# A kernel of attention and a gated feed-forward layer on Trainium2: the product with W2 as seven block products from the second sequence on

## What is computed

```python
# x: (8, 1024, 512) float32; W1, W3: (2048, 512); W2: (512, 2048)
x = x + attention(layernorm(x))        # one head of width 64, causal, rotary, low-rank maps
y = layernorm(x)
hidden = silu(y @ W1.T) * (y @ W3.T)   # 2048 hidden features
hidden = fwht(hidden)                  # Walsh-Hadamard transform over the 2048
x = x + hidden @ W2.T
```

## Time and profile before

| | |
|---|---|
| time, median of 3 runs | 2095.05 us (2094.95 to 2095.1) |
| span of the profiled execution | 2093.3 us |
| around the span, against the median | 1.75 us |
| PE busy | 2049.4 us, 98% |
| DVE busy | 1399.0 us, 67% |
| ACT busy | 932.7 us, 45% |
| POOL busy | 215.0 us, 10% |

### The profile page before, as it was taken

One profiled execution on the slowest core, in us unless ns is written; L12 is line 12 of the kernel. 1 busy time (PEld: TensorE's weight loads), 2 busy tenths in 40 slices (PEclk: granted clock), 3 DMA queues, 4 the chain that ended last, 5 costly groups with the idle time before them and its releaser, 6 DMA issues.

```text
span 2093.3 us, 26809 instructions
## 1 busy us (share of the span) xinstructions
PE 2049.4 (98%) x9846; PEld 986.1 (47%) x9846; DVE 1399.0 (67%) x2674; ACT 932.7 (45%) x1431; POOL 215.0 (10%) x196
## 2 busy tenths in 40 slices
PE   6889999999999999999999999999999999999999
PEld 3534444444444444444444444444444444444444
DVE  7897878667676666766677576766767666743333
ACT  5866455354444444453444444344443445322221
POOL 2354641101001000001001010010100110000000
PEclk8999999999999999999999999999999999999999
DMA  8644246441463333733345423643246332463211
GB/s 336 227 166 174 97 153 153 160 145 60 121 189 111 137 107 95 176 124 116 116 129 161 141 77 106 170 135 130 69 148 154 125 122 92 118 155 108 91 63 68
DMA packets 231138, 278.62 MB, mean 133 GB/s; under 512 B 178016, under 2 KB 178144, under 8 KB 225632
## 3 DMA queue, kind: packets, MB, share of 16 engines
q1 hardware_dynamic: 231008, 276.91, 42.7%
HBM read 194.81 MB, written 39.85 MB: 112 GB/s over the span
## 4 chain that ended last, share of the span: by engine, by line
PE 91%; DVE 4%; ACT 2%; issue 1%; DMA 1%; SPq 0%; POOL 0%; ACTq 0%; DVEq 0%; POOLq 0%
PE PF L926 18%; PE PF L928 17%; PE PF L927 17%; PE PD L988 10%; PE PD L990 10%; PE PD L989 10%; PE XY L747 1%; PE XY L733 1%; PE XY L734 1%; PE XY L757 1%; PE XY L758 1%; PE XY L679 1%; PE XY L678 1%; DMA PT<-Pl 0%; DVE WS L1909 0%
## 5 line engine op out<-in xcount | busy, mean ns | idle before, releaser
L926 PE MATMUL PF<-XF,WS 128*128 128x512 f16 x1778 | 675.3, 380 | 4.1 <-DVE XF L1915 1.9
L928 PE MATMUL PF<-XF,WS 128*128 128x512 f16 x1778 | 673.9, 379 | 0.0
L927 PE MATMUL PF<-XF,WS 128*128 128x512 f16 x1778 | 673.9, 379 | 0.0
L1344 ACT ACTIVATE SH<-PF,afs 128x512 f32<-128x512 f32 x256 | 175.9, 687 | 516.8 <-PE PF L928 514.8
L988 PE MATMUL PD<-W2S,H 128*128 128x512 f16 x1024 | 388.1, 379 | 0.0
L989 PE MATMUL PD<-W2S,H 128*128 128x512 f16 x1024 | 388.1, 379 | 0.0
L990 PE MATMUL PD<-W2S,H 128*128 128x512 f16 x1024 | 388.1, 379 | 0.0
L926 PEld LDWEIGHTS PF<-XF,WS 128*128 128x128 f16 x1778 | 173.8, 98 | 221.6 <-issue 31.0
L928 PEld LDWEIGHTS PF<-XF,WS 128*128 128x128 f16 x1778 | 174.0, 98 | 209.8
L927 PEld LDWEIGHTS PF<-XF,WS 128*128 128x128 f16 x1778 | 174.3, 98 | 186.2 <-issue 4.8
L1950 DVE SCALAR_TENSOR_TENSOR SH<-PF,afs,SH 128x512 f32<-128x512 f32 x256 | 188.8, 747 | 96.8 <-ACT SH L1344 95.0
(11 more groups left out here) (328 smaller groups left out, 2005.2 us busy)
## 6 DMA issues: line engine op xcount, KB each, us to landing
WS<-wscr SPq DMA_DIRECT2D x112, 896.0 KB, 4.9
W2S<-w2scr SPq DMA_DIRECT2D x30, 1024.0 KB, 6.5
ring<-x SPq DMA_DIRECT2D x56, 256.0 KB, 7.1
wscr<-WS SPq DMA_DIRECT2D x16, 896.0 KB, 4.1
out<-ring SPq DMA_DIRECT2D x56, 256.0 KB, 2.3
RAW<-w13t SPq DMA_DIRECT2D x16, 512.0 KB, 4.1
xraw<-xT SPq DMA_DIRECT2D x28, 256.0 KB, 5.4
XF<-w SPq DMA_DIRECT2D x13, 512.0 KB, 18.5
```

The costliest lines, as they stand in the source:

```text
L926: pe.matmul(bank, wh, th, start=i < 2 and j == 0, stop=False, skip_group_check=True)
L927: pe.matmul(bank, wh, tl, start=False, stop=False, skip_group_check=True)
L928: m = pe.matmul(bank, wl, th, start=False, stop=j == 1, skip_group_check=True)
L1344: ac.activation(SH[:, i, :], PF[:, (1 - k % 2, 2)[i], :], ACT.Silu, scale=afs[:, k % NH:k % NH + 1]).then_inc((a_sb, a_sc2)[i], 1)
```

## The change

For the groups of the first sequence (q < `QF` = 4) nothing changes. From q = 4 on the product with W2 is done by seven block products instead of eight. The blocks are: the two hidden tiles of each pair p = k // 2 (q has two pairs, which are two depths of the same sum), the two halves of 512 tokens, and the two halves of 256 features.

- **PE.** `unit(q, u)`, 14 of them for a group (seven products, each for two banks g of 256 tokens), each 12 matmuls of 128x256 with a weight load for each. `UNITS` places three in even steps (positions 1, 3, 6) and four in odd ones (1, 3, 4, 6). A unit waits until the bank of the unit two before it is emptied.
- **Hidden tiles.** The second tile of a pair gets its own buffer SHO (in the space of W2S). `form_sum` on POOL makes four sums of tile halves for a pair, each 128x512, in place; `parts_high` (ACT) and `parts_low` (DVE) split four pieces for a pair, three of 128x1024 and one of 128x512, into H. Before, they split two of 128x1024 for a pair.
- **Results.** Of the 14 units of a group, `take` (ACT) copies 4 into TT, `add_unit` (DVE) adds 4 to TT and 6 to rows of x, and `row_add` (POOL) adds TT to rows, 12 adds of 128x512 in a group. Before, DVE did 8 adds of 128x512 and no other engine had a part in it.
- **W2.** In the first two sequences the sums of W2's blocks are made once (eight rounds of one load, four sums on POOL, one split on ACT and DVE, one store), and `store_w2` issues six more stores each time. From q = 4 on SP loads 256 KB for each of the seven products (three buffers WR) instead of 1 MB for a group.
- **Waits.** `silu` of even steps waits for `parts_low(p - 1, 1)`, the split of the sums, and its second half also for the fourth sum on POOL. Stores of rows come a little later in the sequence.

The core of the diff:

```diff
--- before.py
+++ after.py
+QF = 4
+UNITS = {0: (1, 3, 6), 1: (1, 3, 4, 6), 2: (1, 3, 6), 3: (1, 3, 4, 6)}
+UNIT0 = {0: 0, 1: 3, 2: 7, 3: 10}
+P1, P6, P2, P4, P7, P5, P3 = range(7)
+HFORM = ("A11", "S2", "A12", "A22", "S3", "S1", "S4")
+SPLITS = (("A11", "S3"), ("S1", "S2"), ("A12", "A22"), ("S4",))
+SPLIT_OF = {f: i for i, fs in enumerate(SPLITS) for f in fs}
...
+        SHO = w2s[:, 0:2048].bitcast(F32).rearrange("p (i c) -> p i c", i=2)
+        WR = [w2s[:, o:o + 1024].rearrange("p (r m d) -> p r m d", r=2, m=2) for o in (2048, 3072, 4096)]
+        TT = w2s[:, 5120:7168].bitcast(F32).rearrange("p (g c) -> p g c", g=2)
...
+            def load_form2(n):
+                q, i = QF + n // 7, n % 7
+                if n < 3:
+                    w.wait_ge(p_d, d_no(QF - 2 if n < 2 else QF - 1, 7))
+                else:
+                    w.wait_ge(p_u, 2 * (n - 3) + 2)
+                sp.dma_start(WR[n % 3].rearrange("p r m d -> p (r m d)"), w2f[q % 4, WFILE[i]]).then_inc(d_wf[n % 3], 16)
...
+                    if k > 4 * QF + 3 and unit_at(k, j) and unit_at(k, j)[1] % 2:
+                        n = form_no(unit_at(k, j)[0], unit_at(k, j)[1] // 2) + 3
+                        if n < 7 * (NK // 4 - QF):
+                            load_form2(n)
...
             def down(i):
-                if q < 0:
+                if q < 0 or q >= QF:
...
+            def unit(q, u):
+                i, g, n = u // 2, u % 2, form_no(q, u // 2)
+                bank = PD[:, u % 2, :]
+                w.wait_ge(v_lo, split_no(2 * q + 1, SPLIT_OF[HFORM[i]]))
+                w.wait_ge(d_wf[n % 3], 16 * (n // 3 + 1))
+                if u >= 2:
+                    sem, no = emptied(q, u - 2)
+                    w.wait_ge(sem, no(q, u - 2))
+                elif q == QF:
+                    w.wait_ge(v_ev, d_no(QF - 1, 6 + u))
+                else:
+                    sem, no = emptied(q - 1, u + 12)
+                    w.wait_ge(sem, no(q - 1, u + 12))
+                for tp in range(2):
+                    for r in range(2):
+                        th, tl = (part_of(q, r, HFORM[i], m)[:, (2 * g + tp) * 128:(2 * g + tp + 1) * 128] for m in range(2))
+                        wh, wl = (WR[n % 3][:, r, m, :] for m in range(2))
+                        o = bank[:, tp * 256:(tp + 1) * 256]
+                        pe.matmul(o, th, wh, start=tp == 0 and r == 0, stop=False, skip_group_check=True)
+                        pe.matmul(o, th, wl, start=False, stop=False, skip_group_check=True)
+                        m = pe.matmul(o, tl, wh, start=False, stop=r == 1, skip_group_check=True)
+                m.then_inc(p_u, 1)
...
-                        down(4 * k + DOWN_AT.index(i) - 1)
+                        if k < 4 * QF + 4:
+                            down(4 * k + DOWN_AT.index(i) - 1)
+                        if k == 4 * QF + 3 and i == DOWN_AT[-1]:
+                            down(4 * k + 3)
+                    if unit_at(k, i):
+                        unit(*unit_at(k, i))
...
-            for i in (-1, 0, 2, 1, 3, *range(4, 16)):
-                down(4 * NK + i)
+            for u in range(14):
+                unit(NK // 4 - 1, u)
...
                 w.wait_ge(p_gu, gu_no(k, ((3, 5) if k else (2, 5))[i]))
-                if k:
+                if k > 4 * QF + 1:
+                    p = (k - 3) // 2 if k % 2 else (k - 2) // 2
+                    if k % 2 == 0 and i:
+                        w.wait_ge(g_S, sum_no(p, 3))
+                    n = split_no(p, 3 if k % 2 else 1)
+                    w.wait_ge(a_hi, n)
+                    w.wait_ge(v_lo, n)
                     w.wait_ge(a_hi, k)
                     w.wait_ge(v_lo, k)
...
-                ac.activation(SH[:, i, :], PF[:, (1 - k % 2, 2)[i], :], ACT.Silu, scale=afs[:, k % NH:k % NH + 1]).then_inc((a_sb, a_sc2)[i], 1)
+                ac.activation(sh(k)[:, i, :], PF[:, (1 - k % 2, 2)[i], :], ACT.Silu, scale=afs[:, k % NH:k % NH + 1]).then_inc((a_sb, a_sc2)[i], 1)
...
+            def parts_high(p, i):
+                if i == 2:
+                    w.wait_ge(v_hA, 2 * p + 2)
+                    w.wait_ge(v_hE, 2 * p + 2)
+                else:
+                    w.wait_ge(g_S, sum_no(p, {0: 0, 1: 2, 3: 3}[i]))
+                w.wait_ge(*parts_free(p, i))
+                ac.activation(parts_at(p, i, 0), parts_from(p, i), ACT.Copy).then_inc(a_hi, 1)
+            def take(q, u):
+                w.wait_ge(p_u, unit_no(q, u))
+                if u >= 10:
+                    w.wait_ge(g_r, grow_no(q, 2, u % 2))
+                elif q > QF:
+                    w.wait_ge(g_r, grow_no(q - 1, 3, u % 2))
+                ac.activation(TT[:, u % 2, :], PD[:, u % 2, :], ACT.Copy, scale=afs[:, 65:66]).then_inc(a_T, 1)
...
+                if k > 4 * QF + 2 and k % 2:
+                    parts_high((k - 3) // 2, 3)
                 fill(k, 1)
+                if k > 4 * QF + 1 and k % 2 == 0:
+                    parts_high(k // 2 - 1, 1)
+                take_at(k, 1)
+                if k > 4 * QF and k % 2 and k != 4 * QF + 3:
+                    parts_high(k // 2, 0)
+                if k > 4 * QF + 1 and k % 2 == 0:
+                    parts_high(k // 2 - 1, 2)
...
+            def parts_low(p, i):
+                w.wait_ge(a_hi, split_no(p, i))
+                w.wait_ge(g_S, sum_no(p, (0, 2, 2, 3)[i]))
+                ve.tensor_tensor(parts_at(p, i, 1), parts_from(p, i), parts_at(p, i, 0), ALU.subtract).then_inc(v_lo, 1)
+            def add_unit(q, u):
+                i, g = u // 2, u % 2
+                b, t = PD[:, g, :], TT[:, g, :]
+                w.wait_ge(p_u, unit_no(q, u))
+                if i in (P6, P7):
+                    w.wait_ge(g_r, grow_no(q, 0 if i == P6 else 1, g))
+                    w.wait_ge(a_T, tcopy_no(q, g))
+                    ve.scalar_tensor_tensor(t, b, afs[:, 65:66], t, ALU.mult, ALU.add).then_inc(v_T, 1)
+                else:
+                    r = out_part(q, i in (P4,), 1 if i == P3 else 0, g)
+                    if i == P2:
+                        w.wait_ge(g_r, grow_no(q, 0, g))
+                    elif i == P3:
+                        w.wait_ge(g_r, grow_no(q, 3, g))
+                    elif q > QF:
+                        w.wait_ge(g_r, grow_no(q - 1, 2, g))
+                    ve.scalar_tensor_tensor(r, b.rearrange("p (t c) -> p t c", t=2), afs[:, 65:66], r, ALU.mult,
+                                            ALU.add).then_inc(v_r, 1)
+            def add_at(k, j):
+                if unit_at(k, j) and unit_at(k, j)[1] not in (0, 1, 10, 11):
+                    add_unit(*unit_at(k, j))
...
+                if k == 4 * QF + 4:
+                    parts_low(k // 2 - 1, 0)
                 fill(k, 0)
-                if k:
+                if k and k <= 4 * QF:
                     low_part(k - 1)
+                if k > 4 * QF + 2 and k % 2:
+                    parts_low((k - 3) // 2, 3)
+                add_at(k - 1, 6)
                 fill(k, 1)
                 if k:
                     sum_c(k)
                     out_rows((k - 1) // 4 - 1, 2 * ((k - 1) % 4) + 1)
+                if k > 4 * QF + 1 and k % 2 == 0:
+                    parts_low(k // 2 - 1, 1)
+                add_at(k, 1)
+                if k > 4 * QF and k % 2 and k != 4 * QF + 3:
+                    parts_low(k // 2, 0)
                 fill(k, 2)
+                if k > 4 * QF + 1 and k % 2 == 0:
+                    parts_low(k // 2 - 1, 2)
                 fill(k, 3)
...
+                add_at(k, 3)
                 fill(k, 4)
                 out_rows(k // 4 - 1, 2 * (k % 4))
+                add_at(k, 4)
                 hidden(k, 1)
                 fill(k, 5)
...
             hidden(NK - 1, 0)
-            out_rows(NK // 4 - 2, 7)
-            low_part(NK - 1)
-            for t in range(8):
-                out_rows(NK // 4 - 1, t)
+            add_at(NK - 1, 6)
+            parts_low(NK // 2 - 1, 1)
+            parts_low(NK // 2 - 1, 2)
+            add_unit(NK // 4 - 1, 2)
+            parts_low(NK // 2 - 1, 3)
+            for u in (3, 4, 5, 6, 7, 8, 9, 12, 13):
+                add_unit(NK // 4 - 1, u)
...
+            def form_sum(p, i):
+                A, B = SH, SHO
+                if i == 0:
+                    w.wait_ge(v_hA, 2 * p + 1)
+                    w.wait_ge(v_hE, 2 * p + 1)
+                    o, a, b, op = A[:, 1, :], A[:, 0, :], A[:, 1, :], ALU.subtract
+                elif i == 1:
+                    w.wait_ge(v_hE, 2 * p + 2)
+                    w.wait_ge(a_hi, split_no(p, 0))
+                    w.wait_ge(v_lo, split_no(p, 0))
+                    o, a, b, op = A[:, 1, :], B[:, 1, :], A[:, 1, :], ALU.subtract
+                elif i == 2:
+                    w.wait_ge(g_S, sum_no(p, 1))
+                    o, a, b, op = A[:, 0, :], A[:, 1, :], A[:, 0, :], ALU.add
+                else:
+                    w.wait_ge(a_hi, split_no(p, 2))
```

(28 more changed lines are left out.)

233 lines of the change are left out of this document (199 added, 34 removed).

## The result

| | before | after |
|---|---|---|
| device time, median (fast runs) | 2095.07 us | 2194.58 us (2192.68 to 2197.0, 4 runs) |
| ratio | | 1.0475 (95% interval 1.046 to 1.049) |
| span of the profiled execution | 2093.3 us | 2193.5 us |

What follows compares the result with a forecast made beforehand. PE bounds the kernel by the number and length of its matmuls. 2093.3 - 65 (PE) + 4 (end) + 16 (even steps) + 5 (rest) = 2053 us of span, plus 1.75: 2055 us; 8 in 10 range 2033 to 2098.

Steps and rivals of the forecast that it cites:

- PE: right: Unit matmuls of 256 columns at 0.109 us: a group takes 18.3 instead of 20.7 us, 65 us less in the run.
- Rival 4: Matmuls of 256 columns cost 0.12 us because weight loads show at this length: 2106 us; chance 0.03.
- The end: From the last product to the end, with POOL's last row adds waited for: 4 us longer (3 to 9).
- Loads: Engine loads mid-run: DVE 68% to 77%, 84% with contention; ACT 44% to 54%; POOL 45 to 74%.
- 5 us of contention a group: DVE's sums with two SBUF inputs, half of them beside POOL, add 5 us in four steps; counted into DVE's load.
- DVE in even steps: PE waits before product 6 for DVE's `sum_e`, delayed by two splits: 16 us in all (0 to 41).
- signs of being wrong: The size would be wrong if PE waits for units' banks or `copy_b`, or POOL's operations average 2 us.
- POOL's latency: nothing charged: Seven POOL operations in steps with k % 4 == 3, 8.7 to 14.9 us of 15.5: no cost, waiting adds come later.
- 5 us for everything of its kind: W2 rounds, six more stores, the passage from group 3 to 4, and attention's transposes: 5 us (0 to 10).
- Rival 2: Vector side becomes the bound through fixed-order waits, if mean loss over steps 20 to 111 exceeds 0.6 us; chance 0.11.
- slack of 2 us or more at most hand-overs: The argument against the vector side becoming the bound: most hand-overs between engines have at least 2 us to spare.
- 1.65 times: DVE's sum with two SBUF inputs beside POOL: 2.11 instead of 1.28 us, both engines moving on, each slower.

Runs made afterwards that it cites:

- last_only: The changed kernel with the seven products used for the last sequence's groups alone (`QF = 28`), W2's forms prepared as in the changed kernel: 2112.52 us.
- pool_tiny: The changed kernel with GpSimd's sums of hidden tiles and its row adds on 8 columns, all waits kept: 2097.49 us.
- all_short: The changed kernel with GpSimd's sums and row adds, two of VectorE's four splits a pair, and the operations for W2's halves cut to few columns: 2054.97 us.
- pool_late: The changed kernel with GpSimd's sums and row adds on 8 columns, each with two memsets ahead of it, behind the waits for its inputs: 2098.30 us.
- pool_side: The changed kernel with GpSimd's sums and row adds on 8 columns, each followed by a full scratch addition for which nobody waits: 2141.86 us.

## Why the prediction was wrong

*PE: right.* Unit matmuls start 0.109 us apart, 12 in 1.31 us:

```profile
1050.07 0.27 PE L1196 MATMUL PD<-W2S,H 128*128 128x256 f16 x1
1050.18 0.27 PE L1197 MATMUL PD<-W2S,H 128*128 128x256 f16 x1
...
1051.27 0.27 PE L1198 MATMUL PD<-W2S,H 128*128 128x256 f16 x1
```

Rival 4 is out, and the 2.4 us a group are seen wherever nothing stalls (`last_only`).

*The end: nearly right.* The last product ends at T = 2160.9, the last add at 2188.62 + 0.75 = T + 28.5, forecast T + 27.2; the last adds wait for POOL as described:

```profile
2178.69 9.82 POOL L2584 TENSOR_TENSOR ring<-ring,W2S 128x512 f32<-128x512 f32 x8 [4.65 <-DVE W2S L2240]
```

Against before it is 6 us longer, forecast 4.

*Loads: right.* Forecast for the middle: DVE 77% alone and 84% with contention, ACT 54%, POOL 45 to 74%. Measured: 207.3 / 260 = 80% (with PE stalled; 208.5 us in a sequence of 247 would be 84%), 50%, 51%. The 5 us of contention a group came too: DVE is busy for 208.5 us a sequence in the changed kernel and 188.4 in `pool_tiny`, 5.0 us a group.

*DVE in even steps: right where it was computed.* Before product 6 PE stands 0.5, 0.0, 0.5 and 1.5 us in steps 2, 6, 10 and 14 of a middle sequence, 0.6 in the mean (forecast 0.55), and 0.1 in the mean in the other even steps (forecast 0.15). That it fits so well is in part luck: the slack of 1.4 us that went into it is the mean over 89 waits, and over all 127 sums it is 124.3 / 127 = 1.0. Yet this was the only kind of stall with a price, 16 us. The two that the prediction named as signs of being wrong are both there: waits for `copy_b` (20.8 us in the run) and for units' banks (20.0 behind L2240).

*The step that failed* is "POOL's latency: nothing charged", and with it that the 5 us of contention a group were put into a load and into no wait. With all three engines in fixed order, each waiting for the other two, the loads are no measure: at 80% of DVE PE stands 23 us a sequence. Here is what the runs put in its place: 139.6 us between `after` and `all_short`, of which cutting GpSimd's operations gives back 97 by itself, cutting the two splits 57, the preparation of W2 14 (168 together, since the first two overlap). The preparation had stood with 5 us for everything of its kind.

*Rival 2* named the mechanism and its threshold, a mean of 0.6 us over 92 steps. The loss in middle sequences was 23 / 16 = 1.4 us a step, though not in every step as it had it. It had 0.11, because "slack of 2 us or more at most hand-overs" was read from a kernel in which POOL had nothing to do. A late result and a slowed VectorE draw on the same slack. `pool_late` shows that 1.4 us of lateness alone fit into it; `pool_side`, that the slowing alone costs 44 us; the changed kernel has both, 1.56 us and the slowing, and pays 97. That they share one slack is my reading of these sums.

*The price of contention.* For a DVE sum beside POOL I had 1.65 times; over all of them, beside POOL or not, the token sums came to 1721 / 1279 = 1.35 times, the splits to 1401 / 1228 = 1.14. The Trainium skill (SBUF — State Buffer, Who interferes with whom) says that a VectorE instruction with two inputs from SBUF contends with a GpSimd instruction that reads SBUF, and not with one that only writes, and that one with at most one SBUF input outside certain modes does not contend. The runs agree in each point: 1279 ns beside memsets, 1498 to 1721 beside additions, 746 with an input in PSUM in all kernels. The same section of the Trainium skill calls this contention an exclusive lock, and the prediction answered that the rows show both moving on, each slower. That was a misreading, and the trace agrees with the Trainium skill: the ends 1.08 us apart above are what a lock gives, and the earlier trace rows has the same, DVE's sum ending at 105.06 + 2.11 = 107.17 and POOL's second operation at 104.05 + 4.26 = 108.31, 1.14 later. Both engines are longer than alone because each meets the other in flight; POOL's row adds took 1561 ns in the mean against 9.82 / 8 = 1.23 us in the row above, where DVE does almost nothing.

*What stays open.* How the 97 us divide between slowing and lateness in the changed kernel itself: the two do not add, since each shortens the slack of the other. No version that computes the same was faster than the kernel before. The seven products in the last sequence alone, with the last group in the old way, were not tried; by these numbers they gain 3 x 2.4 = 7 us and pay some 14 for W2's halves. Nor was a kernel tried that gives the row adds or the sums of hidden tiles to another engine than POOL.

## What to carry to other kernels

A change that trades the bound engine's time for work on others has to be priced at each hand-over, not by the others' load: list, for each new wait, how long the result takes in the queue that it stands in, and what stands behind it. Test slack before building: operations on 8 columns with the waits kept (here 2097 us) give the most that a lighter version can bring, and a dummy operation ahead of or behind them tells lateness from contention. Try more than one length: the first one here, 1.4 us, said that lateness is free, and 2.0 us said 78. Where several new costs draw on one slack, count it once.

## What the runs showed that I had not expected

- Lateness has an edge: 1.4 us a result costs 0.8 us of 2097, 2.0 us costs 78.
- A VectorE operation with two inputs from SBUF that meets such an operation of GpSimd stands until it is through: the 128x1024 ones ended 1.08 us after it, whatever was left. POOL's 128x512 ones that met one of DVE's ended 1.12 to 1.15 us after that.
- Waits of 0.9 to 3.1 us on PE brought ten short stretches at 1.2 GHz, some 15 us in all.
- A GpSimd memset of 512 16-bit elements (0.52 us) does not slow VectorE's token sums at all (1279 ns); an addition that wrote the same bytes in 1.04 to 1.22 us does (1498 ns).
- ScalarE's copies and activations kept their length in all of it (581 and 687 ns, before and after).
